# Sums over partitions in a band-attention kernel: products with a matrix of ones instead of round trips through DRAM

## The reference, cut to what matters

```python
xn = layernorm(x)                                     # x: 8 batches of 1024 rows x 512
Q, K, V = (xn @ W + b, split into 16 heads of 64)     # W: 512 x 1024
scores  = where(|i - j| <= 64, Q K^T, 0)              # a band; outside it the score is 0, not -inf
attn    = softmax(scores) @ V
h       = relu((xn @ Win + bin_)[..., None] * W1 + b1)
ffn     = (einsum('btmh,mh->btm', h, W2) + b2) @ Wout + bout
out     = x + attn @ Wo + bo + ffn
```

## Time and profile before

| what | value |
|---|---|
| time, three runs | 2390.14 us median, 2388.98 to 2390.52 |
| the profiled execution | 2387.54 us, its span 2385.8 us |
| PE busy | 2191.7 us, 92% of the span |
| DVE busy | 2038.4 us, 85% |
| ACT busy | 1615.9 us, 68% |
| POOL busy | 913.8 us, 38% |
| 16 DMA engines, queue 1 | 16.1% |

### The profile page before, as it was taken

One profiled execution on the slowest core, in us unless ns is written; L12 is line 12 of the kernel. 1 busy time (PEld: TensorE's weight loads), 2 busy tenths in 40 slices (PEclk: granted clock), 3 DMA queues, 4 the chain that ended last, 5 costly groups with the idle time before them and its releaser, 6 DMA issues.

```text
span 2385.8 us, 43819 instructions
## 1 busy us (share of the span) xinstructions
PE 2191.7 (92%) x14941; PEld 1343.6 (56%) x14941; DVE 2038.4 (85%) x5355; ACT 1615.9 (68%) x4345; POOL 913.8 (38%) x1318
## 2 busy tenths in 40 slices
PE   4666766699999999999999999999999999999997
PEld 2333443456666566666666566666666566666664
DVE  2566665699988999899988999899988999899987
ACT  2455546467777777777777777777777777777765
POOL 2544443254333433244333433244333433244323
PEclk7788888899999999999999999999999999999999
DMA  4122121012111211112111211112111211111111
GB/s 104 31 58 58 40 59 44 25 46 89 32 32 36 81 50 31 37 45 89 32 32 36 80 50 31 37 45 89 32 32 36 80 50 32 36 46 54 32 32 45
DMA packets 75408, 115.02 MB, mean 48 GB/s; under 512 B 9884, under 2 KB 24628, under 8 KB 75188
## 3 DMA queue, kind: packets, MB, share of 16 engines
q1 hardware_dynamic: 74960, 112.20, 16.1%
q10 hardware_dynamic: 228, 0.02, 0.0%
HBM read 87.02 MB, written 25.18 MB: 47 GB/s over the span
## 4 chain that ended last, share of the span: by engine, by line
PE 73%; DVE 13%; DMA 7%; POOL 3%; ACT 2%; issue 1%; SPq 0%; ACTq 0%; DVEq 0%; POOLq 0%
PE ps L1248 34%; PE ps L1263 12%; PE ps L1313 8%; PE ps L1301 8%; PE ps L1234 6%; DMA top_kept<-top 4%; DVE probs L930 3%; DVE acc L958 2%; PE ps L1291 2%; DVE pT_lo L1005 1%; PE ps L1273 1%; DMA top_all<-top_kept 1%; PE ps L1204 1%; PE ps L1285 1%; DVE xn L976 1%
## 5 line engine op out<-in xcount | busy, mean ns | idle before, releaser
L1248 PE MATMUL ps<-xT_hi,w_split 128*128 128x512 f16 x3072 | 995.0, 386 | 142.0 <-DVE acc L958 103.0
L415 POOL TENSOR_SCALAR probs<-probs,inv_l,neg_e 128x256 f32<-128x256 f32 x1024 | 565.3, 568 | 587.2 <-DVE neg_e L949 587.2
L538 ACT ACTIVATE probs<-probs,neg_max 128x256 f32<-128x256 f32 x1024 | 506.0, 496 | 200.5 <-DVE neg_max L937 199.8
L1248 PE MATMUL ps<-xT_lo,w_split 128*128 128x512 f16 x1536 | 592.2, 386 | 0.0
L1248 PEld LDWEIGHTS ps<-xT_hi,w_split 128*128 128x128 f16 x3072 | 304.4, 99 | 502.7 <-DVE acc L958 112.6
L930 DVE CUSTOM_DVE_ANT_0 probs<-ps,mask,unit_s 128x256 f32<-128x256 f32 x1024 | 432.9, 478 | 8.2 <-PE ps L1234 5.7
L958 DVE SCALAR_TENSOR_TENSOR acc<-ps,unit_o,acc 128x512 f32<-128x512 f32 x512 | 370.1, 742 | 50.1 <-PE ps L1263 48.7
L421 POOL TENSOR_TENSOR oT_lo<-o_sum,oT_hi 128x512 f16<-128x512 f32 x128 | 148.3, 1169 | 676.8 <-ACT oT_hi L611 675.8
L593 ACT ACTIVATE pT_hi<-ps 128x512 f16<-128x512 f32 x512 | 276.8, 595 | 189.4 <-PE ps L1313 128.0
L1005 DVE TENSOR_TENSOR pT_lo<-ps,pT_hi 128x512 f16<-128x512 f32 x512 | 323.5, 682 | 13.3 <-ACT pT_hi L593 12.0
L1263 PE MATMUL ps<-wo_split,oT_hi 128*128 128x512 f16 x1024 | 310.1, 385 | 25.2 <-issue 8.3
(11 more groups left out here) (120 smaller groups left out, 3116.9 us busy)
## 6 DMA issues: line engine op xcount, KB each, us to landing
w_split<-w_kept SPq DMA_DIRECT2D x168, 256.0 KB, 2.6
acc<-in_L_attn_x SPq DMA_DIRECT2D x14, 1024.0 KB, 5.6
out_x<-acc SPq DMA_DIRECT2D x14, 1024.0 KB, 4.6
wo_split<-wo_kept SPq DMA_DIRECT2D x56, 256.0 KB, 2.6
w_kept<-w_split SPq DMA_DIRECT2D x24, 256.0 KB, 4.6
acc<-in_L_attn_x SPq DMA_DIRECT2D x4, 512.0 KB, 5.7
w_raw<-in_L_attn_Wv SPq DMA_DIRECT2D x8, 256.0 KB, 4.9
w_raw<-in_L_attn_Wq SPq DMA_DIRECT2D x8, 256.0 KB, 4.8
```

The costliest lines, as they stand in the source:

```text
L415: pool.tensor_scalar(probs[:, h, t], probs[:, h, t], inv_l[:, c:c + 1], neg_e[:, c:c + 1], ALU.mult, ALU.add).then_inc(normed, 1)
L538: act.activation(probs[:, h, t], probs[:, h, t], ACT.Exp, bias=neg_max[:, c:c + 1], accum_out=row_sum[:, c:c + 1])
L1248: last = pe.matmul(dst[:], w[wp][:, i, c], xT[xp][:, c, half * LINE:half * LINE + LINE], start=(c == 0 and a == 0), stop=(c == KC - 1 and ...
```

## The change

The DRAM tensors `top_kept`, `tops_kept` and `bias_kept`, and all transfers from and to them, are gone. PE multiplies `top` (128 x 1 to 128 x 4) by a 128 x 128 matrix of ones: the result in PSUM has the sum over partitions in every partition. A second product adds the squared biases, also summed. DVE reads the sum from PSUM with one instruction. There is now one chain per step: step n finds the scales of the V, Q and K weights of pair n + 1 and of the output weights of pair n - 1 together. `w_scale` has two more rows, since the output weights' scale of a pair now lies two rows further on.

On PE:

```diff
+            def sum_tops(cols, bank, pair, done):
+                out = ps[bank][:, TOP_COLUMN + cols.start:TOP_COLUMN + cols.stop]
+                weights = cols.start < 3
+                last = pe.matmul(out, ones[:], top[:, cols], start=True, stop=not weights, skip_group_check=True)
+                if weights:
+                    biases = slice(cols.start, min(cols.stop, 3))
+                    last = pe.matmul(ps[bank][:, TOP_COLUMN + biases.start:TOP_COLUMN + biases.stop], ones[:],
+                                     bias_squared[:, biases, pair], start=False, stop=True, skip_group_check=True)
+                last.then_inc(done, 1)
+            def sum_step_tops(n, bank):
+                if n < PAIRS - 1:
+                    for i in (V_, Q_, K_):
+                        pe.wait_ge(w_top[i], n + 2)
+                if n > 0:
+                    pe.wait_ge(w_top[3], n)
+                sum_tops(tops_of_step(n), bank, n + 1, top_sum)
...
                     project_qk(1)
+                if 0 < n < PAIRS:
+                    masks_read(1)
+                    sum_step_tops(n, TOP_BANK)
...
+                    if n == PAIRS:
+                        sum_step_tops(n, TOP_BANK)
+                    if n <= PAIRS:
+                        pe.wait_ge(top_ready, scaled_in(n))
                     project_out(3)
...
                     transpose_values(1)
+                if n == 0:
+                    sum_step_tops(n, FIRST_TOP_BANK[0])
```

On DVE:

```diff
+            def read_tops(cols, bank, done, count, ready):
+                dve.wait_ge(done, count)
+                dve.tensor_scalar(top_used[:, cols], ps[bank][:, TOP_COLUMN + cols.start:TOP_COLUMN + cols.stop],
+                                  W_TOP ** -2, (W_FLOOR / W_TOP) ** 2, ALU.mult, ALU.max).then_inc(ready, 1)
+            def step_scales(n):
+                cols = tops_of_step(n)
+                dve.wait_ge(root_ready, scaled_in(n))
+                power_of_two(cols, w_scale[:, n + 1, cols], top_split, w_scaled, scaled_in(n))
+                if n < PAIRS - 1:
+                    biases_and_unit(n + 1)
+                if n > 0:
+                    output_unit(n - 1)
...
-                if attend and n <= PAIRS:
-                    output_tops(j)
                 if out_proj:
                     add_output(0)
...
-                if split_next:
-                    weight_tops(n + 1, V_, K_ + 1)
...
                     qk_low(0)
                 if ffn and k == 0:
                     network_line(0)
-                if attend and n <= PAIRS:
-                    output_scale(j)
+                if 0 < n < PAIRS:
+                    read_tops(tops_of_step(n), TOP_BANK, top_sum, scaled_in(n), top_ready)
...
                     denominators(1)
-                if split_next:
-                    weight_scales(n + 1, V_, K_ + 1)
-                    biases_and_unit(n + 1)
+                if 0 < n <= PAIRS:
+                    step_scales(n)
...
+                if n == 0:
+                    read_tops(tops_of_step(0), FIRST_TOP_BANK[0], top_sum, scaled_in(0), top_ready)
+                    step_scales(0)
                     split_network_out()
```

On ACT (the first lines stood right after `value_lines(0)`):

```diff
-                if attend and n <= PAIRS:
-                    output_top(j)
...
                     exps(1)
...
+                if attend and n <= PAIRS:
+                    output_top(j)
-                if split_next:
+                if split_next and attend:
                     for i in (V_, Q_, K_):
                         weights_top(n + 1, i)
```

On POOL:

```diff
-                if attend and n <= PAIRS:
-                    inverse_root(slice(3, 4), o_top_ready, j + 1, o_root_ready)
                 if attend:
                     normalise_weights(0)
-                if split_next:
-                    inverse_root(slice(0, 3), top_ready, scales_of(n + 1, K_), root_ready)
+                if 0 < n <= PAIRS:
+                    inverse_root(tops_of_step(n), top_ready, scaled_in(n), root_ready)
```

On SP:

```diff
-                    if attend:
-                        share_output_top(k - 1)
-                    if split_next:
-                        share_tops(k + 1)
```

More of the change, by code:

```diff
@@ L176, in scales_of, with output_scales_of, scaled_in, tops_of_step @@
             return 1 if pair == 0 and i == V_ else 2 + pair
-        def tops_of(pair, i):
-            return 1 if pair == 0 and i == V_ else 3 + pair
+        def output_scales_of(pair):
+            return 4 + pair
+        def scaled_in(step):
+            return step + 3
+        def tops_of_step(n):
+            return slice(0 if n < PAIRS - 1 else 3, 4 if 0 < n <= PAIRS else 3)
         def column(tp, h, i):
@@ L367, in _ @@
             pool.memset(minus_half[:], -0.5).then_inc(pool_set, 1)
+            pool.memset(ones[:], 1.0).then_inc(ones_set, 1)
             pool.wait_ge(pool_set, 1)
@@ L480, in output_top @@
                 if pair > 0:
-                    act.wait_ge(o_top_sent, 16 * pair)
+                    act.wait_ge(top_sum, output_scales_of(pair - 1))
                 act.activation(squares[:, 3], wo_raw[:], ACT.Square, accum_out=top[:, 3:4]).then_inc(w_top[3], 1)
@@ L762, in step @@
                         act.wait_ge(wo_got, 16 * j)
-                    act.activation(wo[hi][:], wo_raw[:], ACT.Identity, scale=w_scale[:, j, 3:4]).then_inc(wo_hi, 1)
+                    act.activation(wo[hi][:], wo_raw[:], ACT.Identity, scale=w_scale[:, j + 2, 3:4]).then_inc(wo_hi, 1)
+                if n == 0:
+                    split_high(n + 1, V_)
+                    split_high(n + 1, Q_)
                 if split_next:
@@ L1193, in step @@
                     shift_rows(slice(0, T), b + 3)
-                if ffn and k == 0 and b == 0:
+                if n == 0:
+                    read_tops(tops_of_step(0), FIRST_TOP_BANK[0], top_sum, scaled_in(0), top_ready)
+                    step_scales(0)
                     split_network_out()
@@ L1220, in _ @@
                         last.then_inc(xT_done, 1)
+            pe.wait_ge(w_top[Q_], 1)
+            pe.wait_ge(w_top[K_], 1)
+            sum_tops(slice(1, 3), FIRST_TOP_BANK[1], 0, top_sum)
+            pe.wait_ge(w_top[4], 1)
+            pe.matmul(ps[FIRST_TOP_BANK[2]][:, TOP_COLUMN + 4:TOP_COLUMN + 5], ones[:], top[:, 4:5], start=True, stop=True) \
+                .then_inc(win_top_sum, 1)
             def step(n, b, k, proj=True, attend=True, out_proj=True, split=False, last=False, **_):
```

170 lines of the change are left out of this document (50 added, 120 removed).

## The result

The changed kernel takes 2270.43 us (median of 4 runs, 2269.85 to 2274.45) against 2389.56 for the kernel before in the same comparison. The ratio is 0.9507, with a 95% interval of 0.949 to 0.9523. The forecast was 2290, its range 2250 to 2328: the sign, the range and the main wait held, and the gain came out at 117.7 us of span where 100 had been forecast. The profiled execution has a span of 2268.1.

What follows compares the result with a forecast made beforehand. PE was taken to bound seven batches, nearly all gain lying in its waits in the first 504 us. Savings of 48.5, 31 and 21 sum to 100: 2387.5 becomes 2287.5, with 2.6 for the median 2290; range 2250 to 2328.

Steps and rivals of the forecast that it cites:

- Which wait ends last in steps 2 to 6: Steps 2 to 6: PE would wait, 3 to 12 us, for ACT's squares of the next pair's raw K weights.
- The size of that term: Steps 2 to 6: 44.6 us a step, together 223 against 271.5, saving 48.5.
- The part behind the sum: Steps 2 to 6, after K's squares: products 0.3, project_out(2) to next step 20.5, new guard and slower clock 1.5 us.
- the first term: Steps 2 to 6: raw K lands 21.5 us after the step's start; squares and reading the accumulator take 0.8.
- The load named: Steps 2 to 6: raw K, loaded last, lands late because it shares the engines with stores and loads that stay.
- The rule weighed in the prediction: Raw loads: about 2.0 us plus bytes at 436 GB/s, so every raw K lands some 15 us after step start.
- The start: Up to step 2: first product at about 22, step 2 at 107 to 106 instead of 126.98; saves 21 us (10 to 28).
- Steps 7 and 8: Only output weights' squares are waited for: 75 us against 105.63, saving 31 (24 to 34).
- The clock: Steps 2 to 6: after a long stall PE restarts at the lower clock, unless too short; within a 1.5 us allowance.
- The signs: Expected profile: steps 2 to 6 40 to 48 us, step 5 shortest, PE waits at ones 3 to 12.
- rival 1: Steps 2 to 6: raw K lands early, at 15.0 us, steps 36.6, near PE's own pace; 2250 us; chance 0.12.
- Rival 3: Steps 2 to 6: raw loads block PE's queue, making the kernel slower, 2410 us with landings 24 later; chance 0.03.

Runs made afterwards that it cites:

- The eleventh run: Changed kernel plus, in steps 1 to 6, a 512-byte write of top's output-weights column behind the loads, never read or waited for: 2279.48 us, ratio 0.9576.
- the fifth: Changed kernel with both old DRAM round trips put back, V, Q and K's and the output weights': 2362.09 us, ratio 0.9881.
- the second: Changed kernel with SP storing and reloading weights in the order their splits become ready, x load behind the burst: 2259.52 us, ratio 0.9483.
- seventh runs: Kernel with SP's list in split order, batch 1's stored-weight loads in step 7 back ahead of the output weights' wait: 2250.19 us, ratio 0.9409.
- the eighth run: Changed kernel with two raw V, Q, K buffers, step 0's K split before biases, output-weight split before the attention output's second half: 2238.38 us, ratio 0.9367.
- the first run: Changed kernel with the 1 MB load of x in steps 2 and 3 moved behind the raw V, Q and K loads: 2261.56 us, ratio 0.9501.
- the fourth run: Changed kernel with only V, Q and K's old DRAM round trip put back beside the products in steps 1 to 6: 2299.86 us, ratio 0.9652.
- the ninth: The eighth run's kernel with step 0's sum made earlier and step 1's product behind V's second half: 2236.3 us, ratio 0.9387.

## Why the prediction was right, and where it was off

**Which wait ends last in steps 2 to 6: right.** PE's wait at the product is ended by ACT's squares in all five steps (21.1 us in sum). With the loads a step ahead it is gone, and the steps fall by 22.3 us.

**The size of that term: too small by 12.2.** Saved were 60.7 us (271.50 - 210.76), forecast 48.5. The part behind the sum was right: the products start 22.3 us ahead of the next step in the mean, and 0.3 + 20.5 + 1.5 was forecast. Off was the first term, landing 21.5 and squares 0.8: 22.3 against 19.9 measured, 5 x 2.4 = 12. The step of it that failed is the sentence that none of the neighbours goes away with the change. One does: the 512-byte write of the trip itself, issued right behind the load. The eleventh run shows that such a write makes these loads land later and the kernel 7 to 16 us slower. It is not shown to be all of the 12: the landings came back from 5.9 to 6.8 us in that run and to 6.5 in the fifth, with both trips there, and the kernel before had 8.4. The forecast had the row for it, 303.78 directly behind 302.98, and read only the write's own delay from it.

**The load named: half right.** K lands last in all five steps, as forecast, and its squares end PE's wait. But the burst was read as K's alone. In steps 2 and 3 V takes as long as K from its issue, and ACT waits 5.73 us for V and 0.62 for K in step 2. The reason is one thing that the forecast passed over: V and Q are ready 17 and 11 us before they are stored in step 2, and SP stands at the wait for the output weights' low part. The rule weighed in the prediction gives about 2.6 us for a load of 256 KB, an estimate by the Trainium skill, page "DMA: Bandwidth & Descriptors", section "Anatomy of one DMA — SWDGE (gpsimd) path". The loads come near it where their neighbours are spread out: 2.8 to 3.3 us in the second and seventh runs.

**The start: 28.0 saved, 21 forecast.** The first product came at 21.04 (forecast 22), V of pair 1 was ready 9.97 us after the end of step 0 (forecast 9), 7.57 of them one wait of PE, the rest of step 1 behind V's second half took 19.6 (20.9). K's low part made PE wait 5.55 us in step 1, as forecast. Off was the end of step 0: 48.80 against 56. Of the 7 us, two things make 5.7: the waits of 4.56 for the second half of x and 0.99 for a weight split, in the sum left as they were, became 0.48, 0.51 and 1.22; and with the stall of 6.72 its slow restart went too, V's second half in 5.10 us before and 2.75 after.

**Steps 7 and 8: 77.8 against 75.** The guard costs 1.86 and 2.83 us there, as the timeline shows at 326.45 and 366.92; it had been priced for steps 2 to 6 only.

**The clock: right here, in both directions.** Behind waits of 3.9 us and more the product ran at the lower level, behind 2.33 and 1.61 not. The length of the wait alone does not decide it: behind 4.54 us in step 1 of the eighth run the product took 0.36 us, behind 2.02 in step 5 of the first run 0.53.

**The signs.** PE's waits at the product were 1.61 to 7.30 us, where 3 to 12 had been named, and the steps 36.98 to 45.25 us long and not 40 to 48, with step 5 the shortest as forecast. The errors partly cancel: 12.2 and 7.0 us more saved than forecast in steps 2 to 6 and at the start, 3.2 less in steps 7 and 8.

**The rivals.** The result lies on rival 1's side: raw K landed 13.0 + 5.9 = 18.9 us after a step's start in the mean, where 21.5 was forecast and rival 1 had 15.0. Rival 3's mechanism, PE's own queue held by raw loads, is real at a price of 21 us of waiting; for the other sign it would have needed 118 us more.

## What to carry to other kernels

A small transfer can cost more than its size tells: here 0.5 KB took 7.1 us and more with nothing ahead of it, and 1.5 KB in another form 1.8. Before a late landing is put down to the queue, look for the same transfer where it stands alone; the fifth run's steps 7 and 8 decided it here. And when a transfer goes, ask which others had it as a neighbour. In a queue with waits, list for each entry when its data are ready and when it is issued: here a gap of 17 us, closed by reordering, was worth as much as a second buffer. An item that is moved must be checked against every loop that ends with it: the loads of batch 1's weights, moved by mistake, took back 15 of 21 us.

## What the runs showed of the hardware

- A write to DRAM of 0.5 KB, 4 bytes from each of 128 partitions, landed 7.1 to 8.7 us after its issue with no other transfer of the kernel under way (462.63 before; 393.81 and 444.20 in the fifth run), and 11.3 and 11.7 behind a burst of some 3 MB. One of 1.5 KB, 12 bytes from each partition, landed after 1.8 to 2.6 us in the fourth run. Why is open.
- A write of 1.5 KB took 4.27 us beside a read of `o_top_all` (fifth run, 243.01), 1.81 alone.
- A write issued behind a 256 KB load delayed that load: 10.3 us against 7.5 in step 2, 5.4 against 2.9 in step 1, but 4.3 against 5.5 in step 6. In step 4 it was so in each of the three kernels that have the write. What decides it is open.
- A pair of products with a 128x128 matrix of ones in fp32 (4 and 3 columns, two passes each) takes about 0.43 us at the higher clock level and 0.85 at the lower, by the starts of what follows them (121.83, then 122.25 and 122.68 in step 2).
- Steps differ from kernel to kernel where nothing was edited: step 8 took 40.48 us in the eighth run and 43.39 in the ninth, which differ in steps 0 and 1 alone. A single profile can't tell 3 us in one step.
